# Norm factors and row scales turned into rows by a store and a broadcast load instead of by TensorE transposes

## What is computed

```python
scale = cond @ norm_w.T + 1.0                      # per batch, 512 columns
ms = jnp.mean(x * x, axis=-1, keepdims=True)
h = x * (scale[:, None, :] * jax.lax.rsqrt(ms + EPS))
u = h @ up_w.T                                     # 512 -> 2 * 2048
val, gate = jnp.split(u, 2, axis=-1)
h = val * jax.nn.gelu(gate, approximate=False)
# act_quant: per row, s = 127 / max|h|, round(h * s), clipped, / s
# weight_quant: down_w to -1, 0, 1 times its mean magnitude
y = hq @ wq.T                                      # 2048 -> 512
return y + x
```

## Time and profile before

| | us |
|---|---|
| median of 3 runs | 800.59 |
| lowest, highest | 799.56, 801.91 |
| the profiled execution | 799.94 |
| its span | 798.2 |
| PE busy | 736.0 (92%) |
| DVE busy | 580.2 (73%) |
| ACT busy | 358.6 (45%) |
| POOL busy | 97.2 (12%) |

### The profile page before, as it was taken

How to read it: one execution, slowest core, us unless ns; L and a number is a source line. 1 busy time by engine, 2 the same in 40 slices (tenths; PEclk the granted TensorE clock), 3 DMA queues, 4 the chain that set the end, 5 groups by cost and what they waited for, 6 DMA issues and landing times.

```text
span 798.2 us, 15510 instructions
## 1 busy us (share of the span) xinstructions
PE 736.0 (92%) x6012; PEld 594.5 (74%) x6012; DVE 580.2 (73%) x1147; ACT 358.6 (45%) x726; POOL 97.2 (12%) x127
## 2 busy tenths in 40 slices
PE   2687777689999999999999999999999999999998
PEld 1466566477886888688877888788877888788863
DVE  5888888579876777577866877587857877467747
ACT  4678667454433454145423543155323433234415
POOL 4655441008500000000000000000000000000000
PEclk9899899899999999999999999999999999999999
DMA  6445335837544343524343434534452334354302
GB/s 228 172 160 190 112 136 172 281 109 241 186 140 127 114 139 120 162 91 164 120 153 105 146 107 125 170 109 133 123 163 92 107 101 136 100 151 140 97 28 80
DMA packets 37945, 110.32 MB, mean 138 GB/s; under 512 B 4336, under 2 KB 4336, under 8 KB 36720
## 3 DMA queue, kind: packets, MB, share of 16 engines
q1 hardware_dynamic: 37872, 109.33, 42.2%
HBM read 93.59 MB, written 15.73 MB: 137 GB/s over the span
## 4 chain that ended last, share of the span: by engine, by line
PE 72%; DVE 15%; issue 6%; ACT 5%; POOL 1%; DMA 0%; DVEq 0%; SPq 0%; ACTq 0%; POOLq 0%
PE ps_v L400 14%; PE ps_v L401 14%; PE ps_v L402 14%; PE ps_y L477 12%; PE ps_g L400 6%; PE ps_g L401 6%; PE ps_g L402 6%; DVE h L905 2%; DVE w_lo L786 2%; DVE h L870 2%; ACT g L581 2%; DVE w_lo L779 2%; ACT w_hi L616 2%; DVE h_max L883 1%; DVE rs_t L807 1%
## 5 line engine op out<-in xcount | busy, mean ns | idle before, releaser
L400 PE MATMUL ps_v<-x_hi,w_hi 128*128 128x256 f16 x1280 | 354.7, 277 | 19.9 <-ACT p L566 7.8
L401 PE MATMUL ps_v<-x_lo,w_hi 128*128 128x256 f16 x1280 | 354.5, 277 | 0.0
L402 PE MATMUL ps_v<-x_hi,w_lo 128*128 128x256 f16 x1280 | 354.4, 277 | 0.0
L563 ACT COPY ps_g<-ps_v 128x256 f32<-128x256 f32 x128 | 45.8, 358 | 265.1 <-PE ps_v L402 265.1
L400 PEld LDWEIGHTS ps_v<-x_hi,w_hi 128*128 128x128 f16 x1280 | 127.4, 100 | 46.7 <-ACT p L566 9.7
L858 DVE TENSOR_TENSOR ps_v<-ps_v,p 128x256 f32<-128x256 f32 x128 | 54.8, 428 | 123.6 <-PE ps_v L402 123.5
L401 PEld LDWEIGHTS ps_v<-x_lo,w_hi 128*128 128x128 f16 x1280 | 127.1, 99 | 18.0
L400 PE MATMUL ps_g<-x_hi,w_hi 128*128 128x256 f16 x512 | 139.7, 273 | 0.0
L401 PE MATMUL ps_g<-x_lo,w_hi 128*128 128x256 f16 x512 | 139.6, 273 | 0.0
L402 PE MATMUL ps_g<-x_hi,w_lo 128*128 128x256 f16 x512 | 139.6, 273 | 0.0
L402 PEld LDWEIGHTS ps_v<-x_hi,w_lo 128*128 128x128 f16 x1280 | 127.2, 99 | 16.4
(11 more groups left out here) (100 smaller groups left out, 595.8 us busy)
## 6 DMA issues: line engine op xcount, KB each, us to landing
w_lo<-w_lo_dram SPq DMA_DIRECT2D x112, 448.0 KB, 3.4
q<-in_up_t_dram SPq DMA_DIRECT2D x16, 512.0 KB, 4.0
xt<-in_x_cols_dram SPq DMA_DIRECT2D x8, 1024.0 KB, 4.9
sums<-in_down_t_dram SPq DMA_DIRECT2D x16, 512.0 KB, 4.4
xs<-in_x_rows_dram SPq DMA_DIRECT2D x28, 256.0 KB, 3.7
w_lo_dram<-w_lo SPq DMA_DIRECT2D x16, 448.0 KB, 3.9
res<-in_x_rows_dram SPq DMA_DIRECT2D x26, 256.0 KB, 3.5
out_dram<-res SPq DMA_DIRECT2D x26, 256.0 KB, 2.8
```

The costliest lines, as they stand in the source:

```text
L400: pe.matmul(to, w_hi[:, wh:wh + P], hi, start=start and kt == 0, stop=False, skip_group_check=True)
L401: pe.matmul(to, w_hi[:, wh:wh + P], lo, start=False, stop=False, skip_group_check=True)
L402: last = pe.matmul(to, w_lo[:, wl:wl + P], hi, start=False, stop=(kt == 1), skip_group_check=True)
L563: act.copy(ps_g[:, n % NG, 0:HB], ps_v[:, n % NV, 0:HB]).then_inc(pair_copied, 1)
```

## The change

The four transposes of `spread_rs` (blocks 1 to 7) and of `spread_scale` (blocks 0 to 6) are gone. In their place SyncE stores the 128 x 4 tile to a 2 KB DRAM row, each number to its place in row order, waits for that store, and loads the row into the new SBUF tile `by_row` on all 128 partitions. `norm` and `scaled` read `by_row` in place of `ps_m`. Block 0's norm factors and the last block's row scales keep the transposes. `rsqrt` moves to n = 7 for c = 1 and n = 12 for c = 2, the squares of block 2 to n = 8 to 11, `Q_COUNT` becomes 1, 2, 1, ..., and at j = 3 `seed_gate` goes ahead of `scaled`. `turn_max` waits for less.

```diff
-    Q_COUNT = (2, 1, 1) * 4
+    Q_COUNT = (1, 2, 1) * 4
...
         def rsqrt_at(c):
-            return J // 2 if c == 1 else J if c == 2 else (c - 2) * J + 11
+            return J // 2 - 1 if c == 1 else 12 if c == 2 else (c - 2) * J + 11
 
         def squares_at(c, i):
-            return 3 + i if c == 1 else 12 + i if c == 2 else (c - 2) * J + 6 + i
+            return 3 + i if c == 1 else 8 + i if c == 2 else (c - 2) * J + 6 + i
...
+            def spread_rs(c):
+                sp.wait_ge(rs_ready, c + 1)
+                sp.dma_start(rs_dram[c].rearrange("(i p) -> p i", p=P), rs[:], allow_slow_non_contiguous=True).then_inc(rs_stored, 16)
+
+            def load_rs(c):
+                sp.wait_ge(rs_stored, 16 * c)
+                sp.wait_ge(xn_ready, c * KT)
+                if c >= 3:
+                    sp.wait_ge(scaled_ready, (c - 2) * J)
+                sp.dma_start(by_row[:], rs_dram[c:c + 1].to_broadcast([P, TB])).then_inc(rs_loaded, 16)
+
+            def spread_scale(b):
+                sp.wait_ge(scale_ready, b + 1)
+                sp.dma_start(scale_dram[b].rearrange("(i p) -> p i", p=P), row_scale[:],
+                             allow_slow_non_contiguous=True).then_inc(scale_stored, 16)
+                sp.wait_ge(scale_stored, 16 * (b + 1))
+                sp.wait_ge(xn_ready, min(b + 3, NB) * KT)
+                if b >= 1:
+                    sp.wait_ge(scaled_ready, b * J)
+                sp.dma_start(by_row[:], scale_dram[b:b + 1].to_broadcast([P, TB])).then_inc(scale_loaded, 16)
...
+                if b >= 1 and j == 2:
+                    spread_scale(b - 1)
                 if j == 0 and 1 <= b < NB - 1:
                     load_xt(b + 1)
+                for c in range(1, NB):
+                    if n == rsqrt_at(c):
+                        spread_rs(c)
+                    if n == (rsqrt_at(c) if c < 3 else (c - 1) * J - 1):
+                        load_rs(c)
...
             def turn_max(b):
                 pe.wait_ge(h_max_ready, (b + 1) * J)
-                pe.wait_ge(xn_ready, min(b + 3, NB) * KT)
-                pe.wait_ge(scaled_ready, b * J)
+                if b == 0:
+                    pe.wait_ge(xn_ready, KT)
+                else:
+                    pe.wait_ge(scale_ready, b)
...
-                if 1 <= b and j == 2:
-                    spread_scale(b - 1)
-                for c in range(1, NB):
-                    if n == spread_rs_at(c):
-                        spread_rs(c)
...
             def scaled(b, j):
                 at = h_home(b, j) * TB
-                dve.wait_ge(scale_rows, b + 1)
-                dve.tensor_tensor(h[:, at:at + TB], h[:, at:at + TB], ps_m[:], ALU.mult).then_inc(scaled_ready, 1)
+                if b == NB - 1:
+                    dve.wait_ge(scale_rows, 1)
+                    dve.tensor_tensor(h[:, at:at + TB], h[:, at:at + TB], ps_m[:], ALU.mult).then_inc(scaled_ready, 1)
+                else:
+                    dve.wait_ge(scale_loaded, 16 * (b + 1))
+                    dve.tensor_tensor(h[:, at:at + TB], h[:, at:at + TB], by_row[:], ALU.mult).then_inc(scaled_ready, 1)
...
+                if k == 0 and 1 <= b < NB:
+                    seed_gate(n)
                 for t in tiles:
                     scaled(b - 1, t)
                 if b == 0 and j + 2 < J:
                     weight_scale(j + 2)
-                if n < NJ:
+                if n < NJ and not (k == 0 and b >= 1):
                     seed_gate(n)
```

More of the change, by code:

```diff
@@ L94, in bass_cond_norm_geglu_bitlinear @@
         lo_dram = nc.dram_tensor("w_lo_dram", [J, P, WO], FP16, kind="Internal").ap()
+        rs_dram = nc.dram_tensor("rs_dram", [NB, T // NB], F32, kind="Internal").ap()
+        scale_dram = nc.dram_tensor("scale_dram", [NB, T // NB], F32, kind="Internal").ap()
         w_hi = sb("w_hi", [P, J * WO], FP16)
@@ L108, in bass_cond_norm_geglu_bitlinear @@
         x_lo = sb("x_lo", [P, 2 * XO], FP16)
+        by_row = sb("by_row", [P, TB], F32)
         g = sb("g", [P, 3, TB], F32)
@@ L202, in bass_cond_norm_geglu_bitlinear @@
         rs_rows = sem("rs_rows")
+        rs_stored = sem("rs_stored")
+        rs_loaded = sem("rs_loaded")
+        scale_stored = sem("scale_stored")
+        scale_loaded = sem("scale_loaded")
         xn_ready = sem("xn_ready")
@@ L443, in turn_peak, with spread_rs_first @@
                 turn(j % 2, peak[:, j % 2:j % 2 + 1]).then_inc(w_rows, 1)
[L445 to L450, removed]
+            def spread_rs_first():
+                pe.wait_ge(rs_ready, 1)
                 for i in range(TT):
@@ L461, in turn_max, with spread_scale_last @@
                 last.then_inc(max_rows, 1)
-            def spread_scale(b):
-                pe.wait_ge(scale_ready, b + 1)
+            def spread_scale_last():
+                pe.wait_ge(scale_ready, NB)
                 for i in range(TT):
@@ L494, in _ @@
             turn_peak(0)
-            spread_rs(0)
+            spread_rs_first()
             turn_peak(1)
@@ L530, in _ @@
             down(NB - 2, 2)
-            spread_scale(NB - 1)
+            spread_scale_last()
             down(NB - 2, 3)
@@ L795, in rsqrt @@
                     dve.wait_ge(sumsq_ready, c * TT)
-                if c >= 1:
-                    dve.wait_ge(rs_rows, c)
+                if c == 1:
+                    dve.wait_ge(rs_rows, 1)
+                elif c >= 2:
+                    dve.wait_ge(rs_stored, 16 * (c - 1))
                 dve.tensor_scalar(ms[:], sumsq[:], 1.0 / D, EPS, ALU.mult, ALU.add).then_inc(rs_step, 1)
@@ L820, in norm @@
             def norm(c, kt):
-                dve.wait_ge(rs_rows, c + 1)
                 dve.wait_ge(xt_loaded, (c + 1) * 16)
                 at = kt * B + c // PER_B
-                dve.scalar_tensor_tensor(out=xt[:, kt, :], in0=xt[:, kt, :], scalar=cs[:, at:at + 1], in1=ps_m[:],
-                                         op0=ALU.mult, op1=ALU.mult).then_inc(xn_ready, 1)
+                if c == 0:
+                    dve.wait_ge(rs_rows, 1)
+                    dve.scalar_tensor_tensor(out=xt[:, kt, :], in0=xt[:, kt, :], scalar=cs[:, at:at + 1], in1=ps_m[:],
+                                             op0=ALU.mult, op1=ALU.mult).then_inc(xn_ready, 1)
+                else:
+                    dve.wait_ge(rs_loaded, c * 16)
+                    dve.scalar_tensor_tensor(out=xt[:, kt, :], in0=xt[:, kt, :], scalar=cs[:, at:at + 1], in1=by_row[:],
+                                             op0=ALU.mult, op1=ALU.mult).then_inc(xn_ready, 1)
             def difference(c, k):
@@ L893, in row_scales @@
                 dve.wait_ge(row_step, 3 * b + 3)
+                if b >= 1:
+                    dve.wait_ge(scale_stored, 16 * b)
                 dve.tensor_scalar(row_scale[:], row_rec[:], QMAX, None, ALU.mult).then_inc(scale_ready, 1)
```

2 lines of the change are left out of this document (removed).

## The result

The changed kernel takes 897.56 us (median of 6 runs, 894.27 to 899.93) against 801.01 us for the kernel before on the same chip: a ratio of 1.120 [1.118, 1.123]. The forecast was 802.4 us, and the range ended at 810.

A forecast was written before the change was run, and what follows sets the result against it. TensorE bounds from block 2 on; before that a loop of VectorE, ScalarE, GpSimd and loads. Blocks 0 and 1 +7.6, later blocks -5.8: +1.8 on 799.94 gives 801.7, as median 802.4 us; range 796 to 810.

The forecast's parts named there:

- Step 2: The store and row load replacing the transposes: L = 3 us, load 3.7 us, hidden in blocks 2 to 7.
- L: Landing time of the 2 KB store of 512 separate numbers: taken as 3 us, bounds 1.8 and 6.3 us.
- rival A: SyncE's queue, blocks 2 to 7: store slow (L of 5 us or more), 813 us at L = 6.3; chance 0.20.
- My two signs of being wrong: Block 2 begins less than 4 or more than 11 us later, or the steady period doesn't fall.
- Step 1: Transposes removed, blocks 2 to 7: 11 x 0.44 us, and 1.0 us from the order; -5.8 us in sum.
- Rival D: A set of transposes costs its four busy times, 1.09 us: faster, 795.2 us; chance 0.03.
- Step 3: Block 0: up load 11 held behind the norm-factor store on SyncE; shift +4.0 us, that is L + 1.0.
- Step 4: Late block 0: rsqrt(2) +1.0 us, norm(1) reading SBUF +0.5 us; SyncE's wait there delays nothing.
- Step 5: Start of block 1: VectorE stands 5.9 us for the row of scale(0); shift +4.9 us.
- rival C: Block 0's row scale comes later still, its load sharing DMA engines: slower, 805.4 us with 3 us more; chance 0.10.
- Step 6: Block 1: VectorE reads by_row from SBUF while GpSimd works; +2.7 us, bounds 0 and +5.

The follow-up runs named there:

- the kernel with the quick store: The changed kernel with the store in 128 pieces of 16 B and by_row read straight, so factors meet the wrong rows: 808.07 us, 1.009.

## Why the prediction was wrong

**Step 2 failed, in its size and in what it left out.** The size: L is 8 to 10 us, not 3. I bounded it above by the mean time of a packet, 142 ns, times 32. The packets of this store take some 8 ns each by the trace, and its time lies elsewhere, so a mean over packets of other shapes was no bound. What was left out: I followed only what waits for the store and the instructions held behind it. "For c >= 3 the store of `rs` has four steps" is true of the factors and cost nothing; the `w_lo` load that is issued 0.47 us later, and that "is three steps ahead", is held up beside the store and lost all three steps. That is place one, and the store that nobody reads shows it. It comes five times (blocks 1 to 5), with 5.4 to 6.0 us of gap and 1.6 to 3.0 of slow clock each. Place two is the one I described in rival A: with L = 10.2 against a slack of 2.6, `residual` is late. Nor did I price what a gap does to TensorE's clock.

**Rival A** named the mechanism of place two, its place and the point from which it decides, and gave 813 us for L = 6.3. With L = 9 its own sum gives 802.4 + 2 x 6 + 6 x 3.4 = 835 us. So the size of L explains about 32 of the 95 us that are missing. Most of the others are place one, which is not in the sum, and the slow clock behind both places. My two signs of being wrong both came: block 2 begins more than 11 us late, and the steady period rises.

**Step 1** was right: -1.24 us a block measured, -1.1 forecast, in other parts: 0.87 from the two sets (0.88 forecast), 0.37 from the order (0.2 forecast). Rival D is out.

The steps of blocks 0 and 1 can be read from the kernel with the quick store (L = 1.4). This is how much later than in the kernel before `hidden` starts on VectorE, in us:

| step | quick store | changed kernel | difference |
|---|---|---|---|
| 10 | 5.7 | 12.2 | 6.5 |
| 12 | 6.7 | 13.2 | 6.5 |
| 16 | 7.8 | 14.4 | 6.5 |
| 19 | 4.0 | 14.0 | 10.0 |
| 20 | 10.8 | 25.3 | 14.5 |
| mark of block 3's x load | 15.6 | 38.6 | 23.0 |

**Step 3** was undersized even at L = 1.4: 5.7 us by step 10, where it gives 2.4. The up load landed in 8.5 us (87.40 to 95.9) where I had 5.0. It is the fourth of eight transfers that SyncE, held until 85.06, issues within 6 us; ScalarE stood 6.12 us. Moving the wait to step 9 gave 6.0 back. At L = 8.15 the up load goes out at 94.49, not 89.2.

**Step 4** was nearly right: `norm(1)` cost 1.0 us in steps 10 and 11 (0.5 forecast), and `rsqrt(2)` 1.2 up to step 16 (1.0 forecast). But "SyncE's wait there delays nothing" holds only for a quick store. In the changed kernel SyncE stands from 138.67 to 146.60 behind the store of `rs(2)`, ahead of the loads of down weights, and block 2's x load goes out at 167.19, against 154.98 with the quick store and 147.72 before.

**Step 5**: the store of `scale(0)` took 4.2 us even in 16-byte pieces, behind two down loads, and the row load 4.9: VectorE stood 7.36 us at the quick store, 11.9 at the slow one (one wait for `by_row`), where I had 5.9. So rival C too was real, and came on top rather than instead.

**Step 6** was right in mechanism: `scaled` takes 1.52 us beside GpSimd and 0.69 without it; +4.8 us (10.8 to 15.6), inside my bounds of 0 and 5, above the +2.7 taken.

So at L = 1.4 blocks 0 and 1 cost 15.6 us. The other 23 of the changed kernel's 38.6 are the 6.7 us more of L. By the last column 6.5 come at the store of `rs(1)`, 3.5 at that of `rs(2)`, 4.5 at that of `scale(0)`, and 8 are place one in block 1. Rival A had two of these four.

## What to carry to other kernels

Ask of a new transfer not only who waits for it but what else is in transfer while it runs; before a scattered store goes in, put it into the old kernel with no reader and look at the transfers beside it. Keep each partition's numbers together in the store and change their order where it is cheap or hidden: here in a ScalarE copy. In a stretch with no slack on TensorE a gap costs more than itself: in the four steady blocks 37.5 us of idle time brought 15.6 us of slow clock.

## What the runs showed of the hardware

- 128 stores of 4 B side by side in DRAM land in 9.4 us, with 4 B between them in 4.45, 8 B between them in 3.25 (one transfer each). The kernel's 512 side by side: 8 to 11.
- While such a store runs, a 448 KB load that takes 3.4 us takes 11.6 to 13.8, on whichever queue the store is, while the store's own packets are recorded at some 8 ns each.
- VectorE's multiply with one of its two SBUF inputs read at a 16 B step takes 1087 ns for 128x512 in the mean of 99, against 679 with that input plain in PSUM; ScalarE's copy with that step at its input 1108.
- VectorE's multiply of two SBUF inputs takes up to 1.52 us while GpSimd works, 0.69 otherwise.
- After a gap of 5.8 us TensorE ran part of the next 10 us at the 1.2 GHz level (granted clock 0.75 over them); after one of 3.6 us the clock was 0.83.
